# A graph layer's row scaling: the last block turned tile by tile, a shorter root step, a shared first rounding and split statistics

## The reference

```python
h = maximum(layernorm(x, axis=-1), 0)          # x: 8 x 2048 x 128, f32
HW = einsum('bnf,fo->bno', h, W)               # W: 128 x 128
A_norm = relu((adj + adj.T) * 0.5)             # adj: 2048 x 2048
D = sum(A_norm, axis=1)
d = where(D > 0, D_safe ** -0.5, 0)
L = eye(2048) - d[:, None] * A_norm * d[None, :]
out = x + relu(einsum('nm,bmo->bno', L, HW))
```

## Time and profile before

| | |
|---|---|
| time, median of 3 runs | 402.4 us (402.3 to 402.48) |
| profiled execution | 402.48 us, of which the span of the trace is 400.7 us |
| TensorE busy | 375.3 us, 94% of the span |
| VectorE, ScalarE, GpSimd busy | 312.4, 189.9, 120.2 us |
| first real product | at 63.24 us |
| TensorE's granted clock, mean | 0.996 of full speed |

### The profile page before, as it was taken

One profiled execution on the slowest core, in us unless ns is written; L12 is line 12 of the kernel. 1 busy time (PEld: TensorE's weight loads), 2 busy tenths in 40 slices (PEclk: granted clock), 3 DMA queues, 4 the chain that ended last, 5 costly groups with the idle time before them and its releaser, 6 DMA issues.

```text
span 400.7 us, 6165 instructions
## 1 busy us (share of the span) xinstructions
PE 375.3 (94%) x2146; PEld 201.3 (50%) x2146; DVE 312.4 (78%) x606; ACT 189.9 (47%) x408; POOL 120.2 (30%) x260
## 2 busy tenths in 40 slices
PE   3478888999999999999999999999999999999995
PEld 3378763445444444545454445444544544454454
DVE  2886889887999887999859579967965796679246
ACT  1475986879977777777754134212211221113001
POOL 0499406397698235654411120400000000000000
PEclk9998999999999999999999999999999999999999
DMA  8999999001147222341344039921130122012203
GB/s 257 370 387 386 388 301 253 26 27 55 53 144 224 106 81 71 115 157 54 105 159 132 26 112 345 306 79 54 52 106 2 52 74 85 2 52 80 79 27 106
DMA packets 69567, 55.00 MB, mean 137 GB/s; under 512 B 2848, under 2 KB 58272, under 8 KB 69536
## 3 DMA queue, kind: packets, MB, share of 16 engines
q1 hardware_dynamic: 69536, 54.60, 42.8%
HBM read 39.91 MB, written 14.68 MB: 136 GB/s over the span
## 4 chain that ended last, share of the span: by engine, by line
PE 85%; DVE 7%; DMA 2%; SPq 2%; issue 2%; ACT 0%; DVEq 0%
PE ps L1215 14%; PE ps L1216 14%; PE ps L1221 14%; PE ps L1231 11%; PE ps L1233 10%; PE ps L1232 10%; PE ps L1134 3%; DMA S<-in_adj_dram 2%; PE ps L1169 2%; DVE S L805 2%; SPq L434 2%; PE ps L1267 2%; PE ps L1269 2%; PE ps L1268 2%; DVE S L881 1%
## 5 line engine op out<-in xcount | busy, mean ns | idle before, releaser
L1216 PE MATMUL ps<-S,hbuf 128*128 128x512 f16 x240 | 91.0, 379 | 0.0
L1215 PE MATMUL ps<-S,hbuf 128*128 128x512 f16 x240 | 91.0, 379 | 0.0
L1221 PE MATMUL ps<-S,hbuf 128*128 128x512 f16 x256 | 76.2, 379 | 0.0
L1231 PE MATMUL ps<-S,hbuf 128*128 128x512 f16 x152 | 57.6, 379 | 0.0
L1233 PE MATMUL ps<-S,hbuf 128*128 128x512 f16 x152 | 57.6, 379 | 0.0
L1232 PE MATMUL ps<-S,hbuf 128*128 128x512 f16 x152 | 57.6, 379 | 0.0
L720 ACT ACTIVATE g<-ps 128x512 f16<-128x512 f32 x31 | 18.2, 595 | 68.1 <-DVE ps L904 32.0
L662 ACT ACTIVATE ps<-hbuf,lnt 128x128 f32<-128x128 f32 x104 | 41.7, 448 | 5.0 <-DVE hbuf L797 5.0
L824 DVE SCALAR_TENSOR_TENSOR S<-S,dneg 128x512 f16<-128x512 f32 x54 | 40.7, 768 | 3.7 <-ACT S L681 3.4
L681 ACT ACTIVATE S<-S,dneg 128x512 f16<-128x512 f32 x54 | 37.9, 717 | 6.0 <-DVE S L824 5.8
L1221 PEld LDWEIGHTS ps<-S,hbuf 128*128 128x128 f16 x256 | 25.0, 98 | 30.3 <-DVE S L824 0.3
(11 more groups left out here) (143 smaller groups left out, 697.9 us busy)
## 6 DMA issues: line engine op xcount, KB each, us to landing
S<-in_adj_dram SPq DMA_DIRECT2D x15, 1024.0 KB, 14.1
hbuf<-in_x_dram SPq DMA_DIRECT2D x64, 128.0 KB, 3.5
sums<-in_x_dram SPq DMA_DIRECT2D x32, 256.0 KB, 2.8
out_dram<-sums SPq DMA_DIRECT2D x31, 256.0 KB, 2.3
t_forms<-work SPq DMA_DIRECT2D x24, 256.0 KB, 2.8
S<-t_forms SPq DMA_DIRECT2D x5, 1024.0 KB, 9.7
S<-in_adj_dram SPq DMA_DIRECT2D x2, 512.0 KB, 12.3
S<-t_forms SPq DMA_DIRECT2D x1, 768.0 KB, 9.7
```

The costliest lines, as they stand in the source:

```text
L1215: nc.tensor.matmul(acc, hbuf[:, u, 0, at:at + P], l_hi(t), start=(i == 0), stop=False)
L1216: nc.tensor.matmul(acc, hbuf[:, u, 1, at:at + P], l_hi(t), start=False, stop=False)
L1221: last = nc.tensor.matmul(acc, hbuf[:, u, 0, at:at + P], l_lo(t), start=False, stop=(i == T - 1))
L1231: nc.tensor.matmul(acc, a_hi, b_hi, start=starts, stop=False)
```

## The change

Four places are edited.

1. `turn_last` takes the last block in two halves (`half` 0: `q` 0 and 1; `half` 1: `q` 2 and 3), with the row tiles `k` outside and the two `q` inside. The row tile is complete, and signalled, one by one in the second half. `add_transposed` takes row tiles 0 and 1 as soon as each is there; tiles 2 and 3 still wait for all four, since they write rows that the second half reads. ScalarE's order is again relu first, mirror second, for `k = 0` of this step too.
2. Unit 6's statistics are taken half ahead of the degrees and half behind `dpos`; unit 7's half behind `split_l_lo(0)` and half behind `split_l_lo(1)`.
3. The Newton step is written with one instruction less (`y * -0.5 * y`, times the degree, plus 1.5, times `y`). The first piece's upper part is rounded by two engines: columns 0 to 255 by ScalarE, 256 to 511 by VectorE (`split_first_hi`), with a semaphore of its own that TensorE and `split_l_lo(0)` wait for. The filler counts go from 12 and 7 to 11 and 6.
4. In `multiply_last` TensorE waits for the upper part first and for the lower part only ahead of the third of six matmuls.

```diff
-IDLE_TURNS = (12, 7)
+IDLE_TURNS = (11, 6)
+STAT_BEHIND = (0, 1)
...
-                    nc.scalar.activation(l_hi(t), s_piece(t), ACT.Copy, scale=dneg[:, mt:mt + 1]).then_inc(l_hi_ready, 1)
+                    cols = slice(0, WIDE // 2 if t == 0 else WIDE)
+                    nc.scalar.activation(l_hi(t)[:, cols], s_piece(t)[:, cols], ACT.Copy,
+                                         scale=dneg[:, mt:mt + 1]).then_inc(l_hi_ready, 1)
...
-                    if s < len(steps) - 1 or k:
-                        relu_s(s, k)
+                    relu_s(s, k)
...
-                dve.wait_ge(a_turned, GRP * s + (k + 1 if i < j else GRP))
+                alone = i < j or s == len(steps) - 1 and k < GRP // 2
+                dve.wait_ge(a_turned, GRP * s + (k + 1 if alone else GRP))
...
+            def split_first_hi():
+                mt = piece_of(0)[0]
+                nc.vector.tensor_scalar(l_hi(0)[:, WIDE // 2:WIDE], s_piece(0)[:, WIDE // 2:WIDE], dneg[:, mt:mt + 1], None,
+                                        ALU.mult).then_inc(first_hi_ready, 1)
...
-                    statistics(u)
+                    statistics(u, 0, GRP if u < EARLY else GRP // 2)
...
-            nc.vector.tensor_tensor(t, dsafe[:], y, ALU.mult).then_inc(deg_chain, 1)
+            nc.vector.scalar_tensor_tensor(t, y, -0.5, y, ALU.mult, ALU.mult).then_inc(deg_chain, 1)
...
-            nc.vector.tensor_tensor(t, t, y, ALU.mult).then_inc(deg_chain, 1)
+            nc.vector.tensor_tensor(t, t, dsafe[:], ALU.mult).then_inc(deg_chain, 1)
...
-            dve.wait_ge(deg_chain, 6)
-            nc.vector.tensor_scalar(t, t, -0.5, 1.5, ALU.mult, ALU.add).then_inc(deg_chain, 1)
             dve.wait_ge(deg_chain, 7)
             nc.vector.reciprocal(scale, unscale).then_inc(deg_chain, 1)
-            dve.wait_ge(deg_chain, 8)
-            nc.vector.tensor_tensor(y, y, t, ALU.mult).then_inc(deg_chain, 1)
-            dve.wait_ge(deg_chain, 10)
+            nc.vector.scalar_tensor_tensor(y, t, 1.5, y, ALU.add, ALU.mult).then_inc(deg_chain, 1)
+            dve.wait_ge(deg_chain, 9)
             nc.vector.tensor_scalar(dneg[:], y, scale, -2.0 ** (L_EXP - 64), ALU.mult, ALU.mult).then_inc(d_ready, 1)
+            dve.wait_ge(d_ready, 1)
+            split_first_hi()
             nc.vector.tensor_scalar(dpos[:], y, unscale, 2.0 ** (64 - L_EXP), ALU.mult, ALU.mult).then_inc(d_ready, 1)
-            dve.wait_ge(d_ready, 1)
+            statistics(EARLY, GRP // 2, GRP)
...
-                    for u in stat_at.get(tau, []):
-                        statistics(u)
                     for t in range(LEAD):
                         split_l_lo(t)
+                        if t in STAT_BEHIND:
+                            b = STAT_BEHIND.index(t) * GRP // 2
+                            statistics(EARLY + 1, b, b + GRP // 2)
...
-                for q in range(GRP):
-                    if q == GRP // 2:
+                for half in range(2):
+                    if half:
                         pe.wait_ge(adj_half, 16)
                     for k in range(GRP):
-                        if q == 0:
+                        if half == 0:
                             pe.wait_ge(a_added, GRP * (s - 1) + k + 1)
                         n = GRP * j + k
-                        last = nc.tensor.transpose(ps[:, k, q * P:(q + 1) * P], S[:, GRP * i + q, n * P:(n + 1) * P], ident[:])
-                        if q == GRP - 1:
+                        for q in range(half * GRP // 2, (half + 1) * GRP // 2):
+                            last = nc.tensor.transpose(ps[:, k, q * P:(q + 1) * P], S[:, GRP * i + q, n * P:(n + 1) * P],
+                                                       ident[:])
+                        if half:
                             last.then_inc(a_turned, 1)
...
             def multiply_last(h):
-                pe.wait_ge(g_lo_ready, TILES + h)
+                pe.wait_ge(g_hi_ready, TILES + h)
...
+                    if i == 0:
+                        pe.wait_ge(g_lo_ready, TILES + h)
```

More of the change, by code:

```diff
@@ L310, in gnn_layer @@
         l_hi_ready = sem("l_hi_ready")
+        first_hi_ready = sem("first_hi_ready")
         l_lo_ready = sem("l_lo_ready")
@@ L729, in _ @@
                             take_mirror(p, k)
-                    if s == len(steps) - 1 and k == 0:
-                        relu_s(s, k)
                 for u in h_at.get(s - FRONT, []):
@@ L785, in _, with statistics @@
         def _(dve):
[L786 to L791, removed]
+            def statistics(u, b0=0, b1=GRP):
+                if b0 == 0:
+                    wait_x(dve, u)
+                    if u >= LN_SLOTS:
+                        dve.wait_ge(ln_v_ready, (u - LN_SLOTS) // LN_BATCH + 1)
+                for b in range(b0, b1):
                     last = nc.vector.bn_stats(stats[:, u % LN_SLOTS, b, :], x_buf(u, b, b + 1))
-                last.then_inc(stats_ready, 1)
+                if b1 == GRP:
+                    last.then_inc(stats_ready, 1)
             def split_h_lo(u):
@@ L816, in take_diag @@
                 nc.vector.scalar_tensor_tensor(d, ident[:], dminus[:, mt:mt + 1], d, ALU.mult, ALU.add).then_inc(s_diag, 1)
+            def split_first_hi():
+                mt = piece_of(0)[0]
+                nc.vector.tensor_scalar(l_hi(0)[:, WIDE // 2:WIDE], s_piece(0)[:, WIDE // 2:WIDE], dneg[:, mt:mt + 1], None,
+                                        ALU.mult).then_inc(first_hi_ready, 1)
             def split_l_lo(t):
                 dve.wait_ge(l_hi_ready, t + 1)
+                if t == 0:
+                    dve.wait_ge(first_hi_ready, 1)
                 if t >= T3_FROM:
@@ L1205, in products @@
                     pe.wait_ge(l_hi_ready, t + 1)
+                    if t == 0:
+                        pe.wait_ge(first_hi_ready, 1)
                 if s % 2 == 0 and row_tiles.index(mt % UNITS) + row_tiles.index(mt % UNITS + UNITS) > 2 * i:
```

## The result

The changed kernel takes 403.74 us (median of 8 runs, 403.57 to 403.94), the kernel before 402.51 us beside it (8 runs, 402.3 to 402.69). The ratio is 1.003, with a 95% interval of 1.0021 to 1.0039: slower by 1.2 us, 0.3%, where a gain of 0.82 us was forecast (401.6 us). The span of the profiled execution is 401.8 us, 1.1 more than before.

The account below looks back on a forecast made before the run. TensorE was taken as the bound, busy 375.3 of 400.7 us, so only its waits could give time. Of 0.99 us in front 0.71 remain, plus 0.11 at the tail: 0.82 us off 402.4, 401.6 us, range 401.25 to 402.25.

Parts of the forecast that it names:

- the root step: Newton step between degree sum and `dneg`, one instruction less: put at 0, with 0.1 us as bound above.
- The shared rounding: First piece's upper part rounded by two engines: 0.02 us gained at the first lower matmul, new instruction 0.36 us.
- d + 1.89: First lower-part matmul, counted from `dneg` (d): forecast 1.89 us after it, against 1.91 before.
- the front: Everything ahead of TensorE's first lower-part matmul: 0.97 + 0.02 = 0.99 us sooner.
- the last block: Last block's transposes taken tile by tile: degree sum starts 0.97 us earlier, bound above 1.04 us.
- The tail: Last half tile's product: two of six matmuls ahead of the lower part bring the scaling 0.11 us sooner.
- It took 71.23 - 63.42 = 7.81 us, so it would end at 72.35: GpSimd's group for units 6 and 7, started at 64.54, keeps its duration and ends before ScalarE comes at 72.37.
- the slack of before: Unit 7's lower part ready at 79.77, wanted by TensorE at 80.09 in the kernel before: 0.32 us.
- the rival for slower: GpSimd's group makes unit 7 later still: gain gone at 8.6 us, 403.3 us at 9.5; chance 0.07.
- unit 7 doesn't hold TensorE up: Rival: VectorE's or ScalarE's chain closes up before unit 7, gain 1.10 us, 401.3 us; chance 0.15.
- the clock falls: Rival: TensorE's clock drops in the front with two fillers less, 1 us back, 402.6 us; chance 0.03.
- GpSimd is late: Rival: GpSimd's group takes 0.3 to 0.7 us longer, delaying unit 6; gain 0.1 to 0.5 us; chance 0.23.

Follow-up runs that it names:

- e14: Kernel before with 8 tiny GpSimd instructions right ahead of the product of variance and inverse root; ratio 0.9999 to the kernel before.
- e9: Kernel before with 18 tiny GpSimd instructions ahead of the group of units 6 and 7; ratio 1.0002 to the kernel before.
- e15: Kernel before with 15 tiny GpSimd instructions ahead of the product of variance and inverse root; median 402.65 us, ratio 1.001, runs in two groups.
- e16: Kernel before with 28 tiny GpSimd instructions ahead of the product of variance and inverse root; 404.67 us, ratio 1.0052.
- e1: Kernel before with edit 1 only, the last block's row tiles signalled one by one; 401.71 us, ratio 0.9978 to the kernel before.
- e2: Changed kernel with the statistics of units 6 and 7 put back where the kernel before has them; 401.89 us, ratio 0.9981 to the kernel before.
- e3: Kernel before with only the split of the statistics; 404.68 us, ratio 1.0048 to the kernel before; run again for its trace, ratio 1.0052.
- e6: Changed kernel with four diagonal additions (row tiles 4 to 7) eight slots later; 402.27 us, ratio 0.9993 to the kernel before.
- e5: Changed kernel with the statistics of units 6 and 7 whole and ahead of the degrees; 401.59 us, ratio 0.9975 to the kernel before.
- e12: Changed kernel with 8 tiny GpSimd instructions right ahead of the product that stalls; ratio 1.0029 to the kernel before.
- e13: Changed kernel with 16 tiny GpSimd instructions right ahead of the product that stalls; ratio 1.0027 to the kernel before.
- e4: Changed kernel with the first piece's upper part rounded by ScalarE alone; 403.7 us, ratio 1.0027 to the kernel before.

## Why the prediction was wrong

**What held.** The degree sum was forecast at 59.34 and came at 59.30, waiting for ScalarE; the first addition at 54.86 and came at 54.83. `dneg` follows 1.87 us after it (1.89), so the root step is worth 0.02 us. The shared rounding's new instruction takes 0.35 us (0.36). The Trainium skill, VectorE: DVE Perf Modes, section "The perf-mode tier table", has two columns a cycle for it; the trace agrees, as the price without that rule was 0.48. The first lower matmul came at 63.03 (forecast d + 1.89 = 63.06), `split_l_lo(2)` at d + 3.16 to the hundredth. Without the shift of 0.09 us between the traces the front gained the 0.99 us that were forecast, but two small errors cancel in that: the last block gave 0.92 and not 0.97, and the rest 0.07 and not 0.02. The tail gave 0.10 us. No clock fell, although two fillers were gone: the longest waits between the last block and the first product are 0.41 and 0.40 us, and the granted clock was 1.00 from 54 to 64 us.

**The step that failed** is "It took 71.23 - 63.42 = 7.81 us, so it would end at 72.35". It ended at 74.14. Unit 6 was forecast at 72.37 and came at 74.18, 1.81 us later; behind it ScalarE and VectorE needed 6.97 us to the end of unit 7's lower part (80.46 + 0.69 = 81.15), 6.95 before. A smaller error stands behind it: TensorE started 0.15 us after that part and not 0.06, so the slack of before was 0.23 us and not 0.32. Together 1.90 us, and with the 0.02 by which the chain was longer 1.92, which is 81.30 - 79.38. The front's gain is all there and is paid away at units 6 and 7, as the rival for slower had it, with its break-even of 8.6 us for a group that took 9.64. It had a chance of 0.07.

**Why the size was off.** The duration of a group was taken over from one place to another. I even wrote that 7.81 us already held a slow instance, as if that bounded it. The runs show otherwise. In the kernel before the product of variance and inverse root starts 0.43 us into a lower part of VectorE (68.99, and 68.56 to 69.31) and ends 0.07 us behind it. Held back to 0.56 us into that lower part (e14) or to 0.70 (e9) it still gets in, in e9 only with the diagonal that follows. At 0.75, the end of that lower part, it gets in or doesn't (e15), and at 1.12 it doesn't (e16). From then on it passes over the ends of the next lower parts until no more diagonals stand between them, at about 72.6 (changed) or 73.1 (before). The split statistics bring it one lower part later, 0.67 us into it (69.72, and 69.05 to 69.79), and there it is shut out. Shown are the place (e1, e2, e3), that a bare delay of the same instruction suffices without any other edit (e16), and that without the alternation there is no hold-up (e6). Where exactly the stretch closes is open: in e9 the product came 0.70 us into its lower part and got in, in the changed kernel 0.67 us into the next one and did not. Not shown is why this product is passed over two to four times, while others of the group (lines 574 and 579 of the kernel before, 0.55 and 0.57 us) got in during the very same stretch. The sharpest pair is e9's line 576 and e16's product, both `TENSOR_TENSOR` of 128x8: they start at 69.71 and 69.72, 0.22 and 0.19 us into the same lower part, and take 0.58 and 3.39 us. The Trainium skill, GPSIMD Engine Reference, section "1. Specifications", names the contention with VectorE's two-input instructions; the traces agree that GpSimd is slower beside them (0.20 us in e5, 2.90 here), but that page has no number from which 2.90 us would follow.

Of the rivals, "unit 7 doesn't hold TensorE up" and "the clock falls" were plainly wrong; "GpSimd is late" had the right place and, with 0.3 to 0.7 us for 1.83, a sixth to two fifths of the size.

## What to carry to other kernels

Before work is moved behind a point, ask which small instruction of another engine depends on it, and what that engine shares with its new neighbours: a duration read in one neighbourhood isn't a bound in another. Here moving six small statistics instructions behind the degrees and between the first lower parts turned a gain of 0.7 us (e2) into a loss of 1.2 us, and taking all eight ahead of the degrees (e5), where VectorE had waits anyway, gave 1.0 us. When two chains tie in a forecast, the one on the engine with the less steady durations deserves the weight.

## What the runs showed of the hardware

A GpSimd `TENSOR_TENSOR` of 128x8 elements, which took 0.20 us ahead of the lower parts (e5), took 2.90 us beside VectorE's alternating two-tensor instructions, 3.39 and 3.76 us where it was held back by a little (e16, e15), and ended within 0.1 us of the end of a VectorE instruction. `MEMSET`s of 128x2 in the same stretch cost 0.03 us each (e12, e13). The whole group of 13 took 5.24 us mostly ahead of that stretch (e5), 7.8 us partly in it and 9.6 us further into it, and 7.8 and 9.6 came out the same to within 0.01 us in three kernels each without a delay (before, e1, e2; changed, e3, e4). Several of the group's instructions end just behind one of VectorE's, so that the group falls into step with them: delays of 0.06 and 0.38 us ahead of it vanished. One kernel, e15, had two times, 402.4 to 402.7 and 404.2 to 404.3 us; that this comes from a start on the edge of an opening is argued from its one trace.
